# One maximum and one copy of 1024 columns for both heads of a step, over two adjacent PSUM banks

## The chip, the cores and the metric

The kernel runs on one core of a Trainium2 chip. Its time is that of the device from start to end, in microseconds (us). Five engines work side by side, each through its own list of instructions, and meet only at semaphores: TensorE (PE; its weight loads are shown apart as PEld), VectorE (DVE), ScalarE (ACT), GpSimd (POOL) and SyncE (SP), which issues transfers.

## The reference

The program is a block of cross-attention followed by a mixture of experts, all in 32 bits, on 32 batches of 128 rows of 256 values.

```python
q = hidden_states @ Wq; k = encoder_hidden_states @ Wk; v = encoder_hidden_states @ Wv   # 16 heads of 64
scores = jnp.einsum('bhsd,bhkd->bhsk', q, k) * scale
probs = jax.nn.softmax(scores, axis=-1)
out = jnp.einsum('bhsk,bhkd->bhsd', probs, v)
...
x = x + jnp.tanh(g_xattn[0]) * _L0_xattn_ref(_layernorm(x, axis=-1), ctx_768, ...)
x = x + jnp.tanh(g_ffn[0]) * _L0_ffn_ref(_layernorm(x, axis=-1), ...)    # top 2 of 8 experts
```

## The kernel before

The attention stage goes through 8 groups `g` of 4 batches (512 rows). A group has 8 steps `j`, each for a pair of heads; `u = 8g + j` numbers the steps. The change lies in these 64 steps. The stage of the experts behind them (from L1029 on) isn't touched.

PE's list for step `u` is: Q (six matmuls, L591 to L593, into a bank of `proj`), K (five, L599 to L603), V (five, L471 to L475), the scores of `u` (L514, the two heads taking turns, `score[0]` and `score[1]`), the transposes of the probabilities of `u - 1` (L488, first head 0 into `probT[0]`, then head 1 into `probT[1]`), and the product with the values for `u - 2` (L501). Some steps have more jobs behind that: O0 and O1 in step 1 (the output projection of the group before), XA and XB in step 2 (transposes of `xn2`, L539), LG in step 3, PR in step 4, T0 and T1 in step 7 (L560, the tables of the routing). Group 0 has none of these jobs. Group 7 has no V in steps 6 and 7.

The jobs take the two banks of `proj` in turn. `take_bank` makes a job wait until the job two places ahead of it has been copied out. So where a step has only Q, K and V, the V of a step waits for the copy of its own Q, which ACT makes (`q_sb`, L705, counted in the trace as L675). Q of step 3 waits for ACT's copy of XA, and K of step 5 for DVE's copy of PR (`ranks`, L876). T1 waits for the one-hot rows that POOL builds after `route_slots` (L227 to L230).

DVE's list for a step is: copy of V (`v_sb`, L911), low part of an attention result (`aT_l`, L760), the two maxima (L919, one for each head), the two copies of the transposed probabilities of the step before (L886), then for each head a wait for ACT's exponentials, a reciprocal (L947) and a multiplication (L949). ACT's list is: `q_sb`, `k_sb`, `aT_h`, then four exponentials for head 0 and four for head 1 (L722), each head behind a wait for its maximum. The order of all lists is written out by hand, and the waits alone decide when each instruction starts.

Of the kernel before, what the change touches and what calls it, by code (L numbers as in the profile page):

```python
# [5 lines left out]
P = 128  # L6
# [9 lines left out]
GB = 4  # L16
NG = B // GB
TOK = GB * S
# [42 lines left out]
def jobs_of(has_prev, has_next):  # L61
    out = []
    for j in range(NP):
        out += [("Q", j), ("K", j)]
        if has_next or j < NP - V_AHEAD:
            out += [("V", j)]
        if has_next and j == NP - 1:
            out += [("FA", 0), ("FB", 0)]
        if has_prev:
            out += [(m, 0) for m in MISC_PREV.get(j, [])]  # L70
    return out
# [47 lines left out]
def attention(nc, ctx, sem, x_v, out_v, xn2_v, xn2_dram, ctxT, g_x, g_f, wq, wk, wv, wo, bo, gateT, fc1T, fc2, shared):  # L119

    f32, f32r, i32, u32 = mybir.dt.float32, mybir.dt.float32r, mybir.dt.int32, mybir.dt.uint32
    ALU, ACT, AX = mybir.AluOpType, mybir.ActivationFunctionType, mybir.AxisListType.X

    def sb(name, shape, dt=f32):
        return ctx.enter_context(nc.sbuf_tensor(name, shape, dt))
# [29 lines left out]
    pT = sb("pT", [P, 2, 2, TOK])  # L155
# [8 lines left out]
    negmax = sb("negmax", [P, 2, 8])  # L164
# [14 lines left out]
    def ps(name):  # L179
        return ctx.enter_context(nc.psum_tensor(name, [P, TOK], f32))  # L180

    proj = [ps("proj0"), ps("proj1")]
    score = [ps("score0"), ps("score1")]
    probT = [ps("probT0"), ps("probT1")]
    av = [ps("av0"), ps("av1")]

    (
        s_consts, s_wo_in, s_c_in, s_x_in, s_xr_in, s_small_in, s_zeros_out, s_w_hi,
        s_w_lo, s_tanh, s_bias_o, s_zrow, s_q_ready, s_k_ready, s_v_ready, s_s_ready, s_pt_ready,
        s_av_ready, s_o_ready, s_xt_ready, s_lg_ready, s_pr_ready, s_tb_ready, s_f_ready, s_at_hi,  # L190
        s_f_hi, s_q_done, s_k_done, s_v_done, s_pt_done0, s_pt_done1, s_at_split, s_f_split, s_negmax,
        s_exp, s_p_ready, s_o_done, s_xa_done, s_xb_done, s_lg_done, s_pr_done, s_tb_done, s_stats1,
        s_rstd1, s_xn_ready, s_stats2, s_rstd2, s_xn2_ready, s_mask_ready, s_gdiff, s_gexp,
        s_slot_ready, s_onehot0, s_onehot1, s_onehot_last, s_token, s_cv_ready, s_ck_ready, s_xr_ready, s_x1_out, s_xn2_out, s_w_rest,
# [2 lines left out]
        "consts", "wo_in", "c_in", "x_in", "xr_in", "small_in", "zeros_out", "w_hi",  # L197
        "w_lo", "tanh", "bias_o", "zrow", "q_ready", "k_ready", "v_ready", "s_ready", "pt_ready",
        "av_ready", "o_ready", "xt_ready", "lg_ready", "pr_ready", "tb_ready", "f_ready", "at_hi",
        "f_hi", "q_done", "k_done", "v_done", "pt_done0", "pt_done1", "at_split", "f_split", "negmax",  # L200
        "exp", "p_ready", "o_done", "xa_done", "xb_done", "lg_done", "pr_done", "tb_done", "stats1",
        "rstd1", "xn_ready", "stats2", "rstd2", "xn2_ready", "mask_ready", "gdiff", "gexp",
        "slot_ready", "onehot0", "onehot1", "onehot_last", "token", "cv_ready", "ck_ready", "xr_ready", "x1_out", "xn2_out", "w_rest",
# [250 lines left out]
    def _(pe):  # L454
# [27 lines left out]
        def transpose_probs(u, j):  # L482
            for hh in range(2):
                pe.wait_ge(s_p_ready, 2 * u + hh + 1)
                if not isinstance(u, int) or u > 0:
                    pe.wait_ge((s_pt_done0, s_pt_done1)[hh], u)
                for b in range(GB):
                    last = nc.tensor.transpose(probT[hh][:, b * P:(b + 1) * P], probs[j % 2][:, hh * GB + b, :], ident[:, :])  # L488
                last.then_inc(s_pt_ready, 1)

        def weigh_values(u, j, v_needed):

            pe.wait_ge(s_v_done, v_needed)
            if not isinstance(u, int) or u > 1:
                pe.wait_ge(s_at_split, u - 1)
            pe.wait_ge(s_pt_done0, u + 1)
            pe.wait_ge(s_pt_done1, u + 1)
            for b in range(GB):
                for hh in range(2):
                    cols = slice((j % 4) * P + hh * DH, (j % 4) * P + (hh + 1) * DH)  # L500
                    last = mm(av[j % 2][hh * DH:(hh + 1) * DH, b * P:(b + 1) * P], v_sb[:, j // 4, b, cols],  # L501
                              pT[:, j % 2, hh, b * P:(b + 1) * P], start=True, stop=True)
            last.then_inc(s_av_ready, 1)
# [125 lines left out]
        def wait_warm(count):  # L629
            keep_warm(nc, av[1], wk_h[:, 0:P], wk_h[:, 0:TOK], count)  # L630

        def finish():

            u = 8 * NG
            transpose_probs(u - 1, NP - 1)
            weigh_values(u - 2, NP - 2, u)
            weigh_values(u - 1, NP - 1, u)
            for half in range(2):
                pe.wait_ge(s_tb_done, 2 * NG - 1 + half)
                project_out(proj[half], NG, 2 * half)  # L640
            for half in range(2):
                pe.wait_ge(s_xn2_ready, NG + half)
                pe.wait_ge(s_exp, 16 * NG)
                for k in range(DK):
                    for b in range(2):
                        last = nc.tensor.transpose(score[half][:, (2 * k + b) * P:(2 * k + b + 1) * P],
                                                   xn2[:, 2 * half + b, k * P:(k + 1) * P], ident[:, :])
                last.then_inc(s_xt_ready, 1)
                if half == 0:
                    pe.wait_ge(s_at_split, 8 * NG)  # L650
                wait_warm(3)
                pe.wait_ge(s_xa_done, NG + half)
                pe.wait_ge((s_pt_done0, s_pt_done1)[half], 8 * NG)
                for b in range(2):
                    for k in range(DK):
                        last = mm(probT[half][:, b * E:(b + 1) * E], xn2T[:, k, (2 * half + b) * P:(2 * half + b + 1) * P],
                                  gate_sb[:, k, :], start=(k == 0), stop=(k == DK - 1))
                last.then_inc(s_lg_ready, 1)
                wait_warm(6)
            misc("PR", av[0], NG)  # L660
            wait_warm(24)
            for half in range(2):
                pe.wait_ge(s_o_done, 2 * NG - 1 + half)
                misc(f"T{half}", proj[half], NG)
# [8 lines left out]
    def _(act):  # L673
# [26 lines left out]
        def iteration(g, has_prev, has_next):  # L700
            jobs = jobs_of(has_prev, has_next)
            for j in range(NP):
                u = 8 * g + j
                act.wait_ge(s_q_ready, u + 1)
                high(q_sb[:, :], bank_of(("Q", j), jobs)[:, :], SCALE).then_inc(s_q_done, 1)  # L705
                act.wait_ge(s_k_ready, u + 1)
                high(k_sb[:, :], bank_of(("K", j), jobs)[:, :]).then_inc(s_k_done, 1)

                if j > 2 or (has_prev and j < 2):
                    attention_high(u - 3, j - 3)  # L710
                if has_next and j == NP - 1:
                    for k in range(DK):
                        act.wait_ge(s_f_ready, 2 * g + 3 + k)
                        high(xT_h[:, k, :], bank_of(("FA" if k == 0 else "FB", 0), jobs)[:, :]).then_inc(s_f_hi, 1)
                if has_prev and j == 4:
                    act.wait_ge(s_gdiff, g)
                    nc.scalar.activation(gexp[:, :], gdiff[:, :], ACT.Exp).then_inc(s_gexp, 1)
                for hh in range(2):
                    act.wait_ge(s_negmax, 2 * u + 1 + hh)
                    for b in range(GB):  # L720
                        c = hh * GB + b
                        last = nc.scalar.activation(probs[j % 2][:, c, :], score[hh][:, b * P:(b + 1) * P], ACT.Exp,  # L722
                                                    bias=negmax[:, j % 2, c:c + 1], accum_out=sums[:, j % 2, c:c + 1])
                    last.then_inc(s_exp, 1)
                    if hh == 0 and has_prev and j == 2:
                        act.wait_ge(s_xt_ready, 2 * g - 1)
                        high(xn2T[:, 0, :], bank_of(("XA", 0), jobs)[:, :]).then_inc(s_xa_done, 1)
                    if hh == 0 and has_prev and j == 1:
                        attention_high(u - 2, j - 2)
# [24 lines left out]
    def _(dve):  # L754
        me = Steps(dve, s_dve_self)
        V = nc.vector
# [124 lines left out]

        def probs_out(u, j):

            for hh, pt_done in enumerate((s_pt_done0, s_pt_done1)):
                dve.wait_ge(s_pt_ready, 2 * u + 1 + hh)
                V.tensor_copy(pT[:, j % 2, hh, :], probT[hh][:, :]).then_inc(pt_done, 1)  # L886

        def residual_start(g):
            dve.wait_ge(s_xr_ready, g)
# [12 lines left out]
        def iteration(g, has_prev, has_next):  # L902
            jobs = jobs_of(has_prev, has_next)
            for j in range(NP):
                u = 8 * g + j
                if ("V", j) in jobs:
                    n = (j + V_AHEAD) % NP
# [6 lines left out]
                if has_prev and j == 2:  # L914
                    dve.wait_ge(s_rstd2, g)
                    normalise(xn2, x1, mv2, rstd2, s_xn2_ready)
                for hh in range(2):
                    dve.wait_ge(s_s_ready, 2 * u + 1 + hh)
                    V.tensor_reduce(negmax[:, j % 2, hh * GB:(hh + 1) * GB],  # L919
                                    score[hh][:, :].rearrange("p (i k) -> p i k", i=GB), axis=AX, op=ALU.max,  # L920
                                    negate=True).then_inc(s_negmax, 1)
                if has_next and j == NP - 1:
                    for k in range(DK):
                        dve.wait_ge(s_f_hi, 2 * g + 3 + k)
# [19 lines left out]
                for hh in range(2):  # L944
                    c = slice(hh * GB, (hh + 1) * GB)
                    dve.wait_ge(s_exp, 2 * u + 1 + hh)
                    n = me.mark(V.reciprocal(rsum[:, c], sums[:, j % 2, c]))  # L947
# [396 lines left out]
```

## Time and profile before

| | us |
|---|---|
| median of 3 runs | 1044.95 (1043.86 to 1045.88) |
| the profiled execution, its own time | 1039.82 |
| its span, first to last instruction | 1038.1 |
| PE busy | 993.9 (96%) |
| DVE busy | 682.9 (66%) |
| ACT busy | 477.9 (46%) |
| POOL busy | 482.6 (46%) |

The attention stage fills the first 606 us or so; its end is finished by 650 us, and the experts run from there. A busy PE is one on which some matmul runs. In the rows of the trace, what stands in brackets at the end is the idle time of that engine just before the instruction, and what ended it.

### The profile page before, as it was taken

The page shows a single profiled execution, that of the slowest core. Times are in us where ns is not written, and L with a number is a line of the kernel's source. Part 1 is how long each engine was busy: PE and PEld are TensorE (multiplying, and loading weights), DVE is VectorE, ACT ScalarE, POOL GpSimd, SP SyncE. Part 2 cuts the span into 40 slices and gives each one's busy share as a digit, 9 for nine tenths or more (in the row PEclk, how much of TensorE's full clock was granted, in tenths as well). Part 3 has the DMA queues.
Part 4 walks back from the last instruction along what each step waited for, and adds up shares of the span by engine and source line. Part 5 has one row for each costly group of instructions (what it writes and reads, how often), then busy time and mean ns, then how long its engine had stood idle before and what let it go on. Part 6 is the DMA issues. An engine that isn't in the chain of part 4 may idle for free. (4 is left out here: it accounts for less than half of the span.)

```text
span 1038.1 us, 21103 instructions
## 1 busy us (share of the span) xinstructions
PE 993.9 (96%) x7314; PEld 855.4 (82%) x7314; DVE 682.9 (66%) x1607; ACT 477.9 (46%) x1502; POOL 482.6 (46%) x498
## 2 busy tenths in 40 slices
PE   6999999999999999999999997999999999999995
PEld 5778878878878778878878786799999899999995
DVE  5886895885885885885886866444455555444552
ACT  3664553553553553653553541344353544435351
POOL 7521071071071170270270153385858567585856
PEclk9999999999999999999999998999999999999998
DMA  9201110120020020021002001425345262523525
GB/s 247 84 9 54 42 48 13 40 61 7 34 61 20 20 61 33 8 61 56 4 0 61 3 1 41 133 37 132 61 107 127 62 147 35 132 56 102 122 55 66
DMA packets 49948, 63.42 MB, mean 61 GB/s; under 512 B 5976, under 2 KB 41714, under 8 KB 49906
## 3 DMA queue, kind: packets, MB, share of 16 engines
q1 hardware_dynamic: 37234, 45.41, 14.0%
q0 software_dynamic: 12672, 17.47, 10.0%
q8 instruction: 25, 0.41, 0.2%
q14 instruction: 17, 0.14, 0.0%
HBM read 46.45 MB, written 16.78 MB: 61 GB/s over the span
## 5 line engine op out<-in xcount | busy, mean ns | idle before, releaser
L1252 ACT ACTIVATE hid<-up,b 128x512 f32<-128x512 f32 x128 | 88.0, 687 | 86.2 <-PE up L1203 86.2
L722 ACT ACTIVATE work<-score,negmax 128x128 f32<-128x128 f32 x256 | 90.2, 379 | 80.6 <-DVE negmax L919 80.6
L1131 POOL DMA_INDIRECT out_dram<-eo,index_e x64 | 106.4, 1663 | 19.5 <-issue 18.9
L722 ACT ACTIVATE probs_odd<-score,negmax 128x128 f32<-128x128 f32 x256 | 90.2, 380 | 51.6 <-DVE negmax L919 51.6
L343 POOL TENSOR_SCALAR var<-mv 128x4 f32<-128x4 f32 (+1 forms) x17 | 3.8, 226 | 219.8 <-DVE mv L774 212.3
L1304 DVE TENSOR_TENSOR eo_raw<-down,b 128x256 f32<-128x256 f32 x64 | 25.9, 425 | 121.1 <-PE down L1217 121.1
L1297 DVE TENSOR_TENSOR hid_l<-hid,hid_h 128x512 fp32r<-128x512 f32 x128 | 88.7, 693 | 4.4
L675 ACT ACTIVATE q_sb<-proj 128x512 f32<-128x512 f32 x64 | 38.7, 604 | 108.9 <-PE proj L593 108.9
L1295 DVE CAST hid_h<-hid 128x512 fp32r<-128x512 f32 x128 | 54.7, 427 | 47.9 <-ACT hid L1252 46.2
L1260 ACT ACTIVATE eo<-eo_raw,gate_e 128x256 f32<-128x256 f32 x64 | 30.9, 506 | 118.1 <-DVE eo_raw L1304 118.1
L919 DVE TENSOR_REDUCE negmax<-score 128x4 f32<-128x512 f32 x128 | 81.9, 681 | 2.1 <-PE score L514 2.1
L514 PEld LDWEIGHTS score<-k_sb,q_sb 64*128 64x128 f32 x1024 | 63.0, 189 | 24.6 <-issue 24.6
L886 DVE COPY pT<-probT 128x512 f32<-128x512 f32 x128 | 81.9, 682 | 0.0
L1119 POOL DMA_INDIRECT rows<-xn_rows,index_e x64 | 67.8, 1060 | 25.1 <-issue 19.1
L514 PE MATMUL score<-k_sb,q_sb 64*128 64x128 f32 x1024 | 75.3, 287 | 1.5 <-issue 1.5
L911 DVE COPY v_sb<-proj 128x512 f32<-128x512 f32 x62 | 42.5, 686 | 47.8 <-PE proj L475 47.8
L527 PE MATMUL proj<-w_split,aT_h 128*128 128x256 f32 x256 | 73.2, 286 | 0.2 <-DVE aT_l L760 0.2
L528 PE MATMUL proj<-w_split,aT_h 128*128 128x256 f32 x256 | 72.4, 283 | 0.0
L529 PE MATMUL proj<-w_split,aT_l 128*128 128x256 f32 x256 | 72.4, 283 | 0.0
L1215 PE MATMUL down<-w_h,hid_h 128*128 128x256 f32 x256 | 71.6, 280 | 0.0
L1215 PE MATMUL down<-w_split,hid_h 128*128 128x256 f32 x256 | 71.4, 279 | 0.0
L1216 PE MATMUL down<-w_l,hid_h 128*128 128x256 f32 x256 | 70.9, 277 | 0.0
(217 smaller groups left out, 3067.2 us busy)
## 6 DMA issues: line engine op xcount, KB each, us to landing
w_raw<-fc1T_dram SPq DMA_DIRECT2D x9, 1024.0 KB, 5.3
w_raw<-fc_dram SPq DMA_DIRECT2D x9, 1024.0 KB, 9.3
rows<-x_dram SPq DMA_DIRECT2D x16, 512.0 KB, 4.6
out_dram<-rows SPq DMA_DIRECT2D x8, 512.0 KB, 3.0
xn_rows<-rows SPq DMA_DIRECT2D x8, 512.0 KB, 2.9
c_raw<-ctxT_dram SPq DMA_DIRECT2D x8, 256.0 KB, 3.9
c_raw<-ctxT_dram SPq DMA_DIRECT2D x16, 128.0 KB, 4.5
b<-fc2b_dram SPq DMA_DIRECT2D x9, 128.0 KB, 8.4
```

The lines of the kernel that those rows point to most:

```text
L514: last = mm(score[hh][:, t], q_sb[r, t], k_sb[r, t], start=True, stop=True)
L527: mm(o, aT_h[:, j, t], wo_h[:, j, :], start=(j == 0), stop=False)
L528: mm(o, aT_h[:, j, t], wo_l[:, j, :], start=False, stop=False)
L529: last = mm(o, aT_l[:, j, t], wo_h[:, j, :], start=False, stop=(j == NP - 1))
L722: last = nc.scalar.activation(probs[j % 2][:, c, :], score[hh][:, b * P:(b + 1) * P], ACT.Exp, bias=negmax[:, j % 2, c:c + 1], accum_out=s ...
L886: V.tensor_copy(pT[:, j % 2, hh, :], probT[hh][:, :]).then_inc(pt_done, 1)
L919: V.tensor_reduce(negmax[:, j % 2, hh * GB:(hh + 1) * GB], score[hh][:, :].rearrange("p (i k) -> p i k", i=GB), axis=AX, op=ALU.max, negat ...
L1131: pool.indirect_dma_start(out=out_rows[:, :], out_offset=bass.IndirectOffsetOnAxis(ap=index_e[par][:, half * GB + i:half * GB + i + 1], ax ...
L1215: mm(o, hid_h[:, k, t], w2_h[par][:, k, :], start=(k == 0), stop=False)
L1216: mm(o, hid_h[:, k, t], w2_l[par][:, k, :], start=False, stop=False)
L1252: nc.scalar.activation(hid[m % 2][:, :], up[m % 2][:, :], ACT.Relu, bias=b1[par][:, m:m + 1]).then_inc(s_hid, 1)
L1297: V.tensor_tensor(hid_l[:, m, :], hid[m % 2][:, :], hid_h[:, m, :].bitcast(f32), ALU.subtract).then_inc(s_hid_split, 1)
```

## The change

`score` and `probT` become one PSUM tensor each, of two adjacent banks. The two maxima of a step become one instruction over both banks, the two copies of the transposed probabilities become one, and the semaphores go with them: the maximum waits for the scores of both heads, all exponentials wait for that one maximum, the copy waits for the transposes of both heads. What PE and ACT execute stays the same.

```diff
-    score = [ps("score0"), ps("score1")]
-    probT = [ps("probT0"), ps("probT1")]
+    score_pair = ctx.enter_context(nc.psum_tensor("score", [P, 2, TOK], f32))
+    probT_pair = ctx.enter_context(nc.psum_tensor("probT", [P, 2, TOK], f32))
+    score, probT = ([pair[:, n] for n in range(2)] for pair in (score_pair, probT_pair))
...
                 if not isinstance(u, int) or u > 0:
-                    pe.wait_ge((s_pt_done0, s_pt_done1)[hh], u)
+                    pe.wait_ge(s_pt_done, u)
...
+                act.wait_ge(s_negmax, u + 1)
                 for hh in range(2):
-                    act.wait_ge(s_negmax, 2 * u + 1 + hh)
...
-            for hh, pt_done in enumerate((s_pt_done0, s_pt_done1)):
-                dve.wait_ge(s_pt_ready, 2 * u + 1 + hh)
-                V.tensor_copy(pT[:, j % 2, hh, :], probT[hh][:, :]).then_inc(pt_done, 1)
+            dve.wait_ge(s_pt_ready, 2 * u + 2)
+            V.tensor_copy(pT[:, j % 2, :, :], probT_pair[:, :, :]).then_inc(s_pt_done, 1)
...
-                for hh in range(2):
-                    dve.wait_ge(s_s_ready, 2 * u + 1 + hh)
-                    V.tensor_reduce(negmax[:, j % 2, hh * GB:(hh + 1) * GB],
-                                    score[hh][:, :].rearrange("p (i k) -> p i k", i=GB), axis=AX, op=ALU.max,
-                                    negate=True).then_inc(s_negmax, 1)
+                dve.wait_ge(s_s_ready, 2 * u + 2)
+                V.tensor_reduce(negmax[:, j % 2, :], score_pair[:, :, :].rearrange("p s (i k) -> p (s i) k", i=GB),
+                                axis=AX, op=ALU.max, negate=True).then_inc(s_negmax, 1)
```

On DVE, a plain step before, with the semaphore that each instruction waits for:

```order
L911 COPY v_sb<-proj 128x512 [waits a_av_ready,a_v_ready]
L760 TENSOR_TENSOR aT_l<-av,aT_h 128x512 [waits a_at_hi]
L919 TENSOR_REDUCE negmax<-score 128x4 [waits a_s_ready] x2
L886 COPY pT<-probT 128x512 [waits a_pt_ready] x2
L947 RECIPROCAL rsum<-sums 128x4 [waits a_exp]
L949 TENSOR_TENSOR work<-work,rsum 128x512 [waits a_dve_self]
L947 RECIPROCAL rsum<-sums 128x4 [waits a_exp]
L949 TENSOR_TENSOR work<-work,rsum 128x512 [waits a_dve_self]
```

The same step on DVE in the changed kernel, whose lines are numbered one to three lower:

```order
L910 COPY v_sb<-proj 128x512 [waits a_av_ready,a_v_ready]
L760 TENSOR_TENSOR aT_l<-av,aT_h 128x512 [waits a_at_hi]
L917 TENSOR_REDUCE negmax<-score 128x8 [waits a_s_ready]
L885 COPY pT<-probT 128x1024 [waits a_pt_ready]
L944 RECIPROCAL rsum<-sums 128x4 [waits a_exp]
L946 TENSOR_TENSOR work<-work,rsum 128x512 [waits a_dve_self]
L944 RECIPROCAL rsum<-sums 128x4 [waits a_exp]
L946 TENSOR_TENSOR work<-work,rsum 128x512 [waits a_dve_self]
```

Two pairs of instructions have become one each; what stands before and behind them is as it was.

On ACT, the exponentials of a step before, and the copies of the next step that are queued behind them:

```order
L722 ACTIVATE work,sums<-score,negmax 128x128 [waits a_negmax]
L722 ACTIVATE work,sums<-score,negmax 128x128 x3
L722 ACTIVATE work,sums<-score,negmax 128x128 [waits a_negmax]
L722 ACTIVATE work,sums<-score,negmax 128x128 x3
L675 ACTIVATE q_sb<-proj 128x512 [waits a_q_ready]
```

The same place on ACT in the changed kernel:

```order
L722 ACTIVATE work,sums<-score,negmax 128x128 [waits a_negmax]
L722 ACTIVATE work,sums<-score,negmax 128x128 x7
L675 ACTIVATE q_sb<-proj 128x512 [waits a_q_ready]
L675 ACTIVATE k_sb<-proj 128x512 [waits a_k_ready]
L697 REGISTER_ALU
```

The eight exponentials now stand behind one wait instead of two, and `q_sb` of the next step still stands behind all eight.

## Rows read from the trace of the kernel before

**Rows 1.** The page's first part: engines, busy us, share, instructions

```profile
PE 993.9 (96%) x7314; PEld 855.4 (82%) x7314; DVE 682.9 (66%) x1607; ACT 477.9 (46%) x1502; POOL 482.6 (46%) x498
```

**Rows 2.** PE's waits, 95 to 606 us: total us, times, longest

```profile
PE proj L471 <- ACT q_sb L675: 4.0, 6, 0.7
...
PE proj L591 <- ACT work L675: 2.0, 7, 0.3
```

**Rows 3.** DVE groups by shape: busy us, mean ns of one, idle before

```profile
L919 DVE TENSOR_REDUCE negmax<-score 128x4 f32<-128x512 f32 x128 | 81.9, 681 | 2.1 <-PE score L514 2.1
L886 DVE COPY pT<-probT 128x512 f32<-128x512 f32 x128 | 81.9, 682 | 0.0
...
L938 DVE TENSOR_TENSOR table<-proj,table 128x128 f32<-128x128 f32 x14 | 4.0, 286 | 5.8 <-PE proj L560 5.8
```

**Rows 4.** Timelines (start us, us) of a plain step, group 3, steps 0 and 1

```profile
308.62 0.39 PE L471 MATMUL proj<-wv_h,cv_h 128*128 128x512 f32 x1
...
309.96 0.69 DVE L911 COPY v_sb<-proj 128x512 f32<-128x512 f32 x1 [1.41 <-PE proj L475]
...
311.16 1.28 DVE L919 TENSOR_REDUCE negmax<-score 128x4 f32<-128x512 f32 x2
...
314.68 0.60 ACT L675 ACTIVATE q_sb<-proj 128x512 f32<-128x512 f32 x1
...
315.62 0.39 PE L471 MATMUL proj<-wv_h,cv_h 128*128 128x512 f32 x1
```

**Rows 5.** Timelines of group 0: first matmul of V in steps 1, 2, 3, 7

```profile
30.38 0.49 PE L471 MATMUL proj<-wv_h,cv_h 128*128 128x512 f32 x1 [1.43 <-ACT q_sb L675]
...
37.08 0.50 PE L471 MATMUL proj<-wv_h,cv_h 128*128 128x512 f32 x1 [0.65 <-ACT q_sb L675]
...
44.20 0.39 PE L471 MATMUL proj<-wv_h,cv_h 128*128 128x512 f32 x1
...
72.47 0.39 PE L471 MATMUL proj<-wv_h,cv_h 128*128 128x512 f32 x1
```

**Rows 6.** Timeline of DVE in group 0, steps 1 and 3

```profile
32.92 1.29 DVE L919 TENSOR_REDUCE negmax<-score 128x4 f32<-128x512 f32 x2 [0.39 <-PE score L514]
...
45.95 0.66 DVE L911 COPY v_sb<-proj 128x512 f32<-128x512 f32 x1
```

**Rows 7.** Timelines of ACT and PE, steps 2 and 3: the copy of XA

```profile
263.59 0.61 ACT L675 ACTIVATE work<-proj 128x512 f32<-128x512 f32 x1
...
264.25 0.50 PE L591 MATMUL proj<-xT_h,w_split 128*128 128x512 f32 x1 [0.29 <-ACT work L675]
```

**Rows 8.** Timelines of ACT, DVE and PEld, steps 4 and 5

```profile
280.21 0.21 ACT L722 ACTIVATION_READ_ACCUMULATOR work<-score,negmax 128x1 f32 x1
...
280.60 0.17 DVE L947 RECIPROCAL rsum<-sums 128x4 f32<-128x4 f32 x1
...
281.41 0.28 DVE L876 COPY ranks<-proj 128x128 f32<-128x128 f32 x1
...
281.75 0.19 PEld L599 LDWEIGHTS proj<-ck_h,wk_h 128*128 128x128 f32 x1
```

**Rows 9.** Timelines of DVE and PE, steps 5 and 6

```profile
284.45 0.69 DVE L911 COPY v_sb<-proj 128x512 f32<-128x512 f32 x1 [0.28 <-PE proj L475]
...
285.66 1.28 DVE L919 TENSOR_REDUCE negmax<-score 128x4 f32<-128x512 f32 x2
...
290.11 0.40 PE L471 MATMUL proj<-wv_h,cv_h 128*128 128x512 f32 x1
```

**Rows 10.** Timelines of PE and POOL, step 7: V, the last one-hot row, T1

```profile
297.97 0.50 PE L471 MATMUL proj<-wv_h,cv_h 128*128 128x512 f32 x1 [0.69 <-ACT q_sb L675]
...
304.45 0.57 POOL L230 TENSOR_SCALAR rows<-iota,hl,gates 128x64 f32<-128x64 f32 x1
...
305.13 1.13 PE L560 MATMUL proj<-rows,work 128*128 128x128 f32 x8 [0.45 <-issue]
```

**Rows 11.** Timeline of PE at the end of attention: the last transposes of head 1

```profile
608.45 0.66 PE L488 MATMUL probT<-ident,probs_odd 128*128 128x128 f32 x4 [0.16 <-DVE probs_odd L949]
```

More of the change, by code:

```diff
@@ L190, in attention @@
         s_av_ready, s_o_ready, s_xt_ready, s_lg_ready, s_pr_ready, s_tb_ready, s_f_ready, s_at_hi,
-        s_f_hi, s_q_done, s_k_done, s_v_done, s_pt_done0, s_pt_done1, s_at_split, s_f_split, s_negmax,
+        s_f_hi, s_q_done, s_k_done, s_v_done, s_pt_done, s_at_split, s_f_split, s_negmax,
         s_exp, s_p_ready, s_o_done, s_xa_done, s_xb_done, s_lg_done, s_pr_done, s_tb_done, s_stats1,
@@ L199, in attention @@
         "av_ready", "o_ready", "xt_ready", "lg_ready", "pr_ready", "tb_ready", "f_ready", "at_hi",
-        "f_hi", "q_done", "k_done", "v_done", "pt_done0", "pt_done1", "at_split", "f_split", "negmax",
+        "f_hi", "q_done", "k_done", "v_done", "pt_done", "at_split", "f_split", "negmax",
         "exp", "p_ready", "o_done", "xa_done", "xb_done", "lg_done", "pr_done", "tb_done", "stats1",
@@ L495, in weigh_values @@
                 pe.wait_ge(s_at_split, u - 1)
-            pe.wait_ge(s_pt_done0, u + 1)
-            pe.wait_ge(s_pt_done1, u + 1)
+            pe.wait_ge(s_pt_done, u + 1)
             for b in range(GB):
@@ L652, in finish @@
                 pe.wait_ge(s_xa_done, NG + half)
-                pe.wait_ge((s_pt_done0, s_pt_done1)[half], 8 * NG)
+                pe.wait_ge(s_pt_done, 8 * NG)
                 for b in range(2):
```

## The prediction

> **What bounds the kernel now.** I read the busy shares first: PE is busy for 96% of the span [rows 1], so time is gained or lost only where PE waits. Then PE's own waits in the attention stage. They are few and short: 6 times V waits for ACT's `q_sb` (0.69 us each), 7 times Q of step 3 waits for ACT's copy of XA (0.29 each) [rows 2]. DVE has spare time there, so what it is given back is worth little by itself. The question is who releases PE at these places, and how far from waiting PE is at the others. That is read in the timelines of single steps.
>
> In a plain step [rows 4] V starts at 308.62, DVE's maxima at 311.16, and the next V at 315.62, which waited for nothing. Behind this runs a chain that isn't seen as a wait: first maximum, eight exponentials, `q_sb` of the next step, release of the next V. Here `q_sb` starts at 314.68 and is ready at 315.28. The next V's weight load stands about 0.23 ahead of its matmul, at about 315.39. So the chain is spare by about 0.1 us only. Group 0 shows the same chain where it does bound: from the first maximum at 32.92 [rows 6] to V at 37.08, which waited [rows 5], 4.16 us. In that form V's first matmul holds PE 0.11 longer (0.50 instead of 0.39), since its weights can't be loaded ahead [rows 4, 5].
>
> **What the change costs.** *The merged maximum.* No row shows 1024 columns. A maximum of 512 takes 0.681; 128 columns of another PSUM operation take 0.286 [rows 3], so 384 columns more cost 0.395, or 0.527 for 512, and the merged one should take 1.21. The bounds: 1.19 at one column per ns, and 1.36 if nothing is shared. The exponentials of head 0 were released after 0.68 and are released after 1.21: **0.53 us later in each of 64 steps** (0.51 to 0.68). Head 1's stand in line behind them, so the whole group of eight, and `q_sb` behind it, move by 0.53. The chain from the start of the maximum to V becomes 4.16 + 0.53 = 4.69.
>
> *What DVE gets back.* Two maxima start 1.28 - 0.68 = 0.60 apart [rows 4], though each lasts 0.68; of these 0.60, some 0.53 are columns. So each merge frees 0.06, and two of them 0.12 per step, 8 us over 64 steps, in an engine that isn't the bound. The Trainium skill ("Perfetto Trace Analysis", Optimizing Scalar/DVE Operations) gives about 125 ns of overhead for a DVE operation on PSUM and says that grouping helps if the engine is saturated, but that breaking instructions up helps where an unsaturated one causes bubbles on others. By its 125 ns, DVE would get back 0.25 per step, 16 us in all; the trace's spacing gives half of that; and its second half speaks against this change.
>
> *The wait for both heads.* The scores of the two heads take turns on PE, so the second is ready less than 0.1 after the first, and the merged copy of `probT` starts behind the merged maximum, when both transposes are done. I price both at nothing inside the stage.
>
> Now the places, each with what PE loses.
>
> - *Group 0, +3.4.* V of step 1 comes 0.6 later (0.53, and 0.07 for the second head's scores). From V to the maxima 2.54 pass [rows 4], 2.65 when V itself waited. So six steps of 2.65 + 4.69 = 7.34 replace those from 30.38 to 72.47 [rows 5], which took 42.09: 44.04, +1.95. In step 3 DVE comes late as it is: `v_sb` starts at 45.95 [rows 6], 1.75 behind its V at 44.20 [rows 5], where a plain step has 1.34. To these 0.41 come 0.53 from the step before, less about 0.28 by which that V is late itself: +0.66. The same at step 7, in front of Q of group 1: +0.2. Sum 0.6 + 1.95 + 0.66 + 0.2 = 3.4.
> - *Step 0 to 1 of groups 1 to 7, +0.34 each.* 311.16 + 4.69 = 315.85 instead of 315.62, and 0.11 for the weights.
> - *Step 2 to 3, +0.53 each.* The copy of XA stands on ACT behind the four exponentials of head 0, and PE already waits for it: it ends at 264.20, Q starts at 264.25 [rows 7]. Both move whole.
> - *Step 4 to 5, inside the group.* The fourth exponential of head 0 ends at 280.42, the reciprocal ran at 280.60, the copy of PR 0.81 behind it [rows 8]. Now the exponentials end at 280.95, the reciprocal runs at 280.99, PR is out at 282.09, and the weights of K, which were loaded from 281.75, come at 282.13. With 0.23 less for the load that ran ahead and 0.11 for the stall, K is 0.27 later, and so is V.
> - *Steps 5 to 7, inside the group.* DVE was free 0.28 before `v_sb` at 284.45 [rows 9]; its second reciprocal now comes 0.53 later, so `v_sb` starts at 284.75, +0.30. The next V: 285.96 + 4.69 = 290.65 instead of 290.11, +0.54 and 0.11. At step 7, V was waiting already [rows 10]: +0.18 from DVE and 0.53, +0.71.
> - *What takes it back.* T1 waits for POOL: the last one-hot row ends at 305.02, T1 starts at 305.13 [rows 10]. Without POOL it would follow T0 by about 0.73 less. POOL's rows hang on DVE's `route_slots` in step 5 alone, and these come +0.30 - 0.12 = +0.18. So all that PE lost in steps 4 to 7 (0.71) lies under this wait, but for **+0.18** per group. If that cover were gone, each group would cost 0.53 more, 3.2 us for six.
> - *Group 7 and the end, +1.9.* It has the 0.34 and the 0.53, but no such cover: the last transposes wait for DVE [rows 11]. DVE's second reciprocal of step 6 is about 0.86 late (0.33 and 0.53), the exponentials of step 7 then 1.39, less about 0.34 spare: the last transposes of head 1 and what hangs on them come 1.05 later than before.
>
> Sum: 3.4 + 6 x (0.34 + 0.53 + 0.18 = 1.05) + 0.87 + 1.05 = **11.6 us**. The experts' stage has none of these instructions and only starts later. Against the profiled execution's own 1039.82 that is 1051.4; the median of the runs lies 5.1 above that execution, and 1044.95 + 11.6 = **1056.5**.
>
> **The rivals.** 0.2%, or 2.1 us, is about what a measurement of this kernel can tell from no change.
>
> *Only the waits that exist grow.* If the 0.1 spare in the plain step is really 0.5 (a release that is faster than the rows' ends suggest), V of step 1 and of the plain steps of group 0 keeps its place: 1.5 in group 0, 7 x 0.53 = 3.7 for XA, 6 x 0.18, and 1 at the end: +7.3, 1052. For it: the ends of PE's rows are modelled. Against: [rows 5] show the chain bounding in two steps of group 0 with the same length.
>
> *Dearer.* If a merged maximum takes 1.36, the 0.53 becomes 0.68 at about 20 places, +3; if POOL's cover is thinner, up to 3 more; if PE's longer pauses lower its granted clock, some more again: 1060 to 1063.
>
> *No change.* ACT is busy for 46% only [rows 1], and 0.53 might vanish in its idle time. Against: it idles before the exponentials, not behind them, where `q_sb` follows at once. Time 1045.
>
> *Faster.* DVE's backlog, not the exponentials, might decide. In steps 4 to 7 it does so in part: `route_slots` would come earlier by two merges, 0.12 by the spacing, up to 0.30 if each frees 0.15 (its whole fixed part, 0.681 - 0.53), and T1 with it. Seven times 0.30 are 2.1 us: 1042.8. It decides only if exponentials released up to 0.53 later cost nothing, so where the merged maximum lasts no longer than 0.68 + 0.30, that is under 0.98, double the column rate of [rows 3]. The Trainium skill's page "VectorE: DVE Perf Modes" (The perf-mode tier table) gives `tensor_reduce` one rate only, which speaks against it; no row here shows another.
>
> **How the numbers follow.** My forecast, 1053.5 to 1059.5: 0.50. Only the existing waits, 1047 to 1053.5: 0.20. Dearer, above 1059.5: 0.17. No change: 0.08. Faster: 0.05. So slower by over 0.2%: 0.87, within: 0.08, faster: 0.05. The range takes in the forecast, most of the cheaper case from 1050 and of the dearer one to 1062.
>
> **What would show it.** In the profile after: one maximum per step near 1.21 us, and the first exponential that much behind its start; PE's wait for `q_sb` no longer in 6 of these places but in nearly all plain steps of group 0 and in steps 1, 6 and 7 of each group; the wait for XA at 0.82 instead of 0.29; T1's wait nearly gone; a group of 8 steps 1.05 us longer; the experts' stage as long as before. I am wrong if V after a plain step still starts without a wait, if the merged maximum is far from 1.21, or if PE's clock shows in it.

## The result, and the profile after

The changed kernel takes 1056.96 us (median of 4 runs, 1055.4 to 1057.49), the kernel before 1044.5 beside it (4 runs, 1043.86 to 1045.88). The ratio is 1.0117, with a 95% interval of 1.0105 to 1.013: 12.5 us slower, where 11.6 was forecast. The profiled execution took 1055.4 us, with a span of 1053.3.

The page's first part, and from its costliest groups the merged instructions and the exponentials (busy us, mean ns of one, and behind the bar the idle time before them):

```profile
PE 1001.8 (95%) x7314; PEld 852.5 (81%) x7314; DVE 679.4 (64%) x1479; ACT 475.7 (45%) x1502; POOL 482.8 (46%) x498
...
L722 ACT ACTIVATE work<-score,negmax 128x128 f32<-128x128 f32 x256 | 90.2, 379 | 95.9 <-DVE negmax L917 95.9
...
L917 DVE TENSOR_REDUCE negmax<-score 128x8 f32<-128x1024 f32 x64 | 77.8, 1216 | 1.0 <-PE score L514 0.9
L885 DVE COPY pT<-probT 128x1024 f32<-128x1024 f32 x64 | 77.8, 1216 | 0.1
```

DVE executes 128 instructions fewer and is busy for 3.5 us less [rows 1]. PE executes as many as before and is busy for 7.9 us more, since a busy PE includes matmuls whose weights come late and those at a lower clock; 3.1 of these us lie within what two executions of the kernel before differ by (993.9 and 997.0). What the change did has to be read from the waits and from single steps, as before.

PE's waits from 95 to 606 us, which answer to [rows 2]:

```profile
PE proj L591 <- ACT work L675: 5.8, 7, 0.8
PE proj L472 <- ACT q_sb L675: 4.4, 12, 0.5
```

and one line of the same view before, which is gone after:

```profile
PE proj L560 <- issue: 2.7, 6, 0.5
```

The wait for XA grew from 2.0 to 5.8 us in the same seven places, 0.54 in each. V waits for `q_sb` in 12 places instead of 6. The wait of T1 (L560) is gone. But all waits that PE shows there add up to about what they did before (10.9 us instead of 10.2), so these lines alone don't give the loss: part of it is in matmuls that are held for less than the view lists, and part was a wait that moved.

A plain step, step 0 of group 4, in the timeline (start, duration, engine). It is the step of [rows 4], which stand under group 3 but are of group 4 too:

```profile
313.74 0.39 PE L472 MATMUL proj<-wv_h,cv_h 128*128 128x512 f32 x1
...
316.28 1.22 DVE L917 TENSOR_REDUCE negmax<-score 128x8 f32<-128x1024 f32 x1
317.53 0.37 ACT L722 ACTIVATE work<-score,negmax 128x128 f32<-128x128 f32 x1 [2.50 <-DVE negmax L917]
...
320.29 0.64 ACT L675 ACTIVATE q_sb<-proj 128x512 f32<-128x512 f32 x1
320.98 0.50 PE L472 MATMUL proj<-wv_h,cv_h 128*128 128x512 f32 x1
```

The merged maximum takes 1.22 us, and the chain from its start to the next V is 320.98 - 316.28 = 4.70. V to V is 7.24, where it was 7.00 [rows 4] (over groups 1 to 6, 7.23 and 7.02), and V's first matmul takes 0.50 instead of 0.39: its weights came with it, not ahead of it.

The V's of group 0, and the DVE multiplication of its first step:

```profile
28.76 2.81 DVE L946 TENSOR_TENSOR work<-work,rsum 128x512 f32<-128x512 f32 x1
29.05 0.50 PE L472 MATMUL proj<-wv_h,cv_h 128*128 128x512 f32 x1 [2.01 <-ACT q_sb L675]
36.77 0.50 PE L472 MATMUL proj<-wv_h,cv_h 128*128 128x512 f32 x1 [1.65 <-ACT q_sb L675]
...
52.08 0.50 PE L472 MATMUL proj<-wv_h,cv_h 128*128 128x512 f32 x1 [0.73 <-ACT q_sb L675]
59.44 0.50 PE L472 MATMUL proj<-wv_h,cv_h 128*128 128x512 f32 x1
66.80 0.50 PE L472 MATMUL proj<-wv_h,cv_h 128*128 128x512 f32 x1
74.18 0.50 PE L472 MATMUL proj<-wv_h,cv_h 128*128 128x512 f32 x1
```

From step 4 on they stand 7.36 to 7.38 apart. V of step 3, at 44.07, comes 7.30 behind that of step 2, and from it to V of step 4 pass 8.01, where 8.00 were forecast (7.34, and 0.66 for DVE, which is late there). V of step 3 and the V's from step 5 on start without a listed wait, yet each first matmul takes 0.50: a chain can bound where no wait is shown.

XA in step 2 of group 3, which answers to [rows 7]:

```profile
267.23 0.37 ACT L722 ACTIVATE work<-score,negmax 128x128 f32<-128x128 f32 x1 [3.69 <-DVE negmax L917]
268.62 0.61 ACT L675 ACTIVATE work<-proj 128x512 f32<-128x512 f32 x1
...
269.28 0.50 PE L591 MATMUL proj<-xT_h,w_split 128*128 128x512 f32 x1 [0.83 <-ACT work L675]
```

Step 7 of that group, which answers to [rows 10]. T0 and T1 are the 16 matmuls of L560:

```profile
303.65 0.50 PE L472 MATMUL proj<-wv_h,cv_h 128*128 128x512 f32 x1 [0.50 <-ACT q_sb L675]
...
309.38 0.58 POOL L231 TENSOR_SCALAR rows<-iota,hl,gates 128x64 f32<-128x64 f32 x1
...
309.19 2.05 PE L560 MATMUL proj<-rows,work 128*128 128x128 f32 x16
311.15 0.47 PE L591 MATMUL proj<-xT_h,w_split 128*128 128x512 f32 x1
```

POOL's last row is ready at 309.96, while T0 still runs, and T1 follows T0 in one stretch. PE is so late by itself that POOL is no longer waited for.

The end of the attention stage, which answers to [rows 11], with the first matmul of the output projection after and before, then PE by the microsecond there (length, PE's busy us and matmuls, granted clock, DMA share, GB/s), then the last copy before the experts:

```profile
616.90 0.66 PE L489 MATMUL probT<-ident,probs_odd 128*128 128x128 f32 x4 [1.29 <-DVE probs_odd L946]
618.29 0.66 PE L489 MATMUL probT<-ident,probs_odd 128*128 128x128 f32 x4 [0.74 <-DVE probs_odd L946]
...
622.42 0.39 PE L527 MATMUL proj<-w_split,aT_h 128*128 128x256 f32 x1
```

```profile
611.64 0.36 PE L527 MATMUL proj<-w_split,aT_h 128*128 128x256 f32 x1 [0.21 <-DVE aT_l L760]
```

```profile
616.00:617.00 1.00, 0.10 (x1) 1.00 0.00 0
617.00:618.00 1.00, 0.55 (x4) 1.00 0.00 0
618.00:619.00 1.00, 0.71 (x6) 1.00 0.00 0
619.00:620.00 1.00, 1.00 (x12) 0.50 0.00 0
```

```profile
659.10 0.29 DVE L1273 TENSOR_TENSOR table<-table,keep 128x128 f32<-128x128 f32 x1 [0.34 <-PEq L102]
```

From the last transposes to the output projection 4.13 us pass; before the change they were 3.19. PE was busy for 1.36 us from 616 to 619, where it had been busy for 1.65 from 606 to 609 before the change. The granted clock then stood at 0.50, the 1.2 GHz level, from 619 to 622 us; it was 1.00 all through this place before.

### The profile page after: what moved, and what is told of

Same layout as the page of the kernel before. It is cut to its first block and busy times, and to the rows that moved or that the text cites. A ratio compares the mean times of both kernels' runs of the same rounds, so it can differ in the third digit from the quotient of the medians.

```text
span 1053.3 us, 20823 instructions
## 1 busy us (share of the span) xinstructions
PE 1001.8 (95%) x7314; PEld 852.5 (81%) x7314; DVE 679.4 (64%) x1479; ACT 475.7 (45%) x1502; POOL 482.8 (46%) x498
## 5 line engine op out<-in xcount | busy, mean ns | idle before, releaser
L722 ACT ACTIVATE work<-score,negmax 128x128 f32<-128x128 f32 x256 | 90.2, 379 | 95.9 <-DVE negmax L917 95.9
L917 DVE TENSOR_REDUCE negmax<-score 128x8 f32<-128x1024 f32 x64 | 77.8, 1216 | 1.0 <-PE score L514 0.9
L885 DVE COPY pT<-probT 128x1024 f32<-128x1024 f32 x64 | 77.8, 1216 | 0.1
L501 PE MATMUL av<-pT,v_sb 128*64 128x128 f32 x1024 | 71.5, 283 | 0.0
```

The lines of the kernel that those rows point to most:

```text
L885: V.tensor_copy(pT[:, j % 2, :, :], probT_pair[:, :, :]).then_inc(s_pt_done, 1)
L917: V.tensor_reduce(negmax[:, j % 2, :], score_pair[:, :, :].rearrange("p s (i k) -> p (s i) k", i=GB), axis=AX, op=ALU.max, negate=True).th ...
```

## The experiments

Each kernel was timed beside the kernel before, whose median was 1045.76 (only the maxima, only the copies, early, late), 1045.39 (the release alone, and the three with XA's copy moved) and 1045.68 (the kernel before again). Gains and losses in us are the ratio less one, times 1045.4; by that measure the changed kernel is 12.2 slower. "The six groups" is the time from Q of group 1 to Q of group 7 in the profiled execution; it is 455.33 before and 461.11 in the changed kernel. It holds six whole groups and nothing of the start and the end, and repeated to 0.3 us when the kernel before was profiled again.

### Only the maxima merged

`splits(j)` gives the ends of the pieces in which the eight blocks of a step go through the maximum: `[8]` is one merged instruction, `[4, 8]` two as before.

```diff
+def splits(j):
+    return [8]
...
+                ends = splits(j)
...
-                    act.wait_ge(s_negmax, 2 * u + 1 + hh)
...
+                        if c == 0 or c in ends:
+                            act.wait_ge(s_negmax, 8 * u + min(e for e in ends if e > c))
...
-                for hh in range(2):
-                    dve.wait_ge(s_s_ready, 2 * u + 1 + hh)
-                    V.tensor_reduce(negmax[:, j % 2, hh * GB:(hh + 1) * GB],
...
+                c0 = 0
+                for c1 in splits(j):
+                    dve.wait_ge(s_s_ready, 2 * u + (1 if c1 <= GB else 2))
+                    V.tensor_reduce(negmax[:, j % 2, c0:c1],
...
+                    c0 = c1
```

> Only the two maxima are merged; the two copies of the transposed probabilities stay apart. Theory (the exponentials are released 0.53 us later, and PE waits for what stands behind them on ScalarE): all of the loss is here, +11 to +13 us on the 1044.5 of the kernel before, so 1055.5 to 1057.5; PE's wait at step 2 (the copy of XA) is 0.83 instead of 0.29. Rival (the merged copy, which waits for both heads' transposes, carries a good part): at most +7, below 1052.

Measured: 1058.74 us, ratio 1.012 (1.0104 to 1.0135), 12.5 us slower; the six groups take 462.64. PE's waits, 95 to 606 us:

```profile
PE proj L476 <- ACT q_sb L680: 5.9, 12, 0.7
PE proj L596 <- ACT work L680: 5.8, 7, 0.8
```

The merged maximum alone gives the whole loss and the whole pattern of waits. V waits somewhat more than in the changed kernel, 0.49 against 0.37 in each of 12 places. That makes 1.5 us, and the six groups are 1.53 longer here than in the changed kernel: so much the merged copies give back.

### Only the copies merged

The maxima use the same `splits`, with `[4, 8]` in every step.

```diff
-            for hh, pt_done in enumerate((s_pt_done0, s_pt_done1)):
-                dve.wait_ge(s_pt_ready, 2 * u + 1 + hh)
-                V.tensor_copy(pT[:, j % 2, hh, :], probT[hh][:, :]).then_inc(pt_done, 1)
+            dve.wait_ge(s_pt_ready, 2 * u + 2)
+            V.tensor_copy(pT[:, j % 2, :, :], probT_pair[:, :, :]).then_inc(s_pt_done, 1)
```

> Only the two copies are merged; the maxima stay apart. Theory: VectorE gets 0.06 us back per step and nothing waits longer inside the stage, so 1043.5 to 1045 (0 to -1 us), with at most 0.5 lost at the end where the copy waits for the second head. Rival (the merged copy carries a good part): +4 or more, 1048.5 and above.

Measured: 1044.44 us, ratio 0.9991 (0.9981 to 1.0): 0.9 us faster, which the interval doesn't tell from nothing. The six groups take 453.95, 1.4 less than before, 0.23 per group. I had allowed for 0.06 of each merge in DVE's list. PE waits in the same places, for `q_sb` 0.25 less in each of six:

```profile
PE proj L564 <- issue: 2.8, 6, 0.5
PE proj L476 <- ACT q_sb L679: 2.5, 6, 0.4
PE proj L595 <- ACT work L679: 2.1, 7, 0.3
```

T1 (now L564) waits for POOL as long as before, and POOL's last row ends 40.54 us behind Q of step 3 in group 3, where it was 40.77. The rows hang on DVE's `route_slots`, whose first two instructions are a sum and a product that run beside POOL. In this kernel, in group 3:

```profile
285.30 0.21 DVE L855 TENSOR_TENSOR place<-ranks,running 128x64 f32<-128x64 f32 x1
285.54 1.20 DVE L857 TENSOR_TENSOR place<-place,mask 128x64 f32<-128x64 f32 x1
```

In the kernel before:

```profile
288.05 1.33 DVE L849 TENSOR_TENSOR place<-ranks,running 128x64 f32<-128x64 f32 x1
289.42 0.23 DVE L851 TENSOR_TENSOR place<-place,mask 128x64 f32<-128x64 f32 x1
```

1.56 became 1.41. So a shift by 0.06 also let the first instruction in ahead of a neighbour on POOL (`cv_d`, from 288.01 before and from 285.32 here), and these 0.15 with the 0.06 are about the 0.23.

Group 0 gives part of the gain back: from V of step 1 to Q of group 1 it takes 48.48 instead of 47.93. Of that, 0.4 lie between V of step 3 and V of step 4 (7.49 instead of 7.09), where DVE is idle for 0.15 and 0.25 us among its statistics. The same 7.46 to 7.49 stand in the two other kernels that merge the copies and keep two maxima in step 3 (late, and copies with XA's copy moved). The profile names no releaser for most of it, and the cause was not traced; the prediction had put the merged copy at nothing.

The "faster" rival of the prediction had the mechanism right, DVE's backlog through `route_slots`, but it decides only while the exponentials aren't late.

### The release alone

Nothing is merged; ACT's exponentials wait for both maxima.

```diff
                 for hh in range(2):
-                    act.wait_ge(s_negmax, 2 * u + 1 + hh)
+                    act.wait_ge(s_negmax, 2 * u + 2)
```

> The kernel before, with two maxima and two copies as they were, but ScalarE waits for both maxima before the first exponential. Nothing is merged; the release alone moves, by the 0.60 us from one maximum's start to the next. Theory (the release of the exponentials sets the loss): at least the loss of the merged maximum, +12 to +15 us, and a wait for the copy of XA of 0.29 + 0.60 = 0.89. Rival (it is the instruction over two banks that costs, by itself or against other engines): under +3.

Measured: 1060.93 us, ratio 1.0142 (1.0127 to 1.0158), 14.8 us slower; the six groups take 465.02. The waits:

```profile
PE proj L591 <- ACT work L675: 6.3, 7, 0.9
PE proj L471 <- ACT q_sb L675: 6.2, 12, 0.7
```

This is the run that isolates the cause: DVE's work is that of the kernel before, to the instruction, and the loss is all there. It is larger than in the changed kernel because two maxima end 1.28 us after the first one starts, the merged one after 1.22, and because the copies give nothing back. A rival by which a reduction over two banks is itself slow, or disturbs PE's writes, is not needed.

### The maximum merged in steps 0 to 3, and in steps 4 to 7

Both are the kernel with only the copies merged, but for one line, so the copies are merged in all steps.

```diff
 def splits(j):
-    return [4, 8]
+    return [8] if j < 4 else [4, 8]
```

> Copies merged in every step, maxima merged in steps 0 to 3 of each group only. Theory: what PE loses ahead of step 4 stays lost: 0.3 at V of step 1 and 0.53 at the copy of XA in each of 7 groups, 5.9, and about 2.2 in group 0: +8 us, 1052.5 (1051 to 1054). Rival (each of the 64 merged maxima costs the same): half of the full loss, +6, and the same as its counterpart in steps 4 to 7.

```diff
 def splits(j):
-    return [4, 8]
+    return [8] if j >= 4 else [4, 8]
```

> Copies merged in every step, maxima merged in steps 4 to 7 of each group only. Theory: inside a group the loss of steps 4 to 7 lies under the wait of T1 for GpSimd's one-hot rows, so only 0.1 to 0.2 per group are left, 1 us for six, 1 in group 0, 1 at the end of the attention stage and up to 1.2 more where PE's clock is granted at half there: +3.2 us, 1047.7 (1046 to 1049.5). Rival (each merged maximum costs the same): +6, 1050.5, as much as in steps 0 to 3.

Measured: early 1053.36, ratio 1.0075 (1.0061 to 1.0089), +7.8 us; late 1048.88, ratio 1.0036 (1.0022 to 1.0049), +3.8 us. The waits of the early kernel:

```profile
PE proj L595 <- ACT work L679: 5.8, 7, 0.8
PE proj L564 <- issue: 2.7, 6, 0.5
PE proj L476 <- ACT q_sb L679: 2.7, 6, 0.5
```

and of the late one:

```profile
PE proj L476 <- ACT q_sb L679: 4.4, 12, 0.5
PE proj L595 <- ACT work L679: 2.0, 7, 0.3
```

The two halves have the waits that the places demand: XA's wait belongs to the early steps, and only the late steps make T1's wait for POOL vanish. Over the six groups, against the kernel with only the copies merged, early costs 4.95 (458.90 - 453.95), late 2.08 (456.03 - 453.95), both together 7.16 (461.11 - 453.95). They add up to 7.03. The early loss is not taken back by T1's wait, because steps 5 to 7 and POOL's work move with it; 4.95 / 6 = 0.83 is about the 0.32 of step 1 and the 0.53 of XA. The late loss is 0.35 per group, of which the merged copies pay back 0.23, which leaves 0.12 against the kernel before. Between Q of step 3 and V of step 7 these groups lose 0.67, and behind V of step 7 they win 0.57 back, where T1 no longer waits for POOL.

### The copy of XA ahead of the exponentials

If late exponentials hurt at XA only because ACT's copy stands behind four of them, the place in ACT's list is what sets the price. The edit is the same in three kernels: the changed one, the one before, and the one with only the copies merged.

```diff
+                if has_prev and j == 2:
+                    act.wait_ge(s_xt_ready, 2 * g - 1)
+                    high(xn2T[:, 0, :], bank_of(("XA", 0), jobs)[:, :]).then_inc(s_xa_done, 1)
                 act.wait_ge(s_negmax, u + 1)
...
-                    if hh == 0 and has_prev and j == 2:
-                        act.wait_ge(s_xt_ready, 2 * g - 1)
-                        high(xn2T[:, 0, :], bank_of(("XA", 0), jobs)[:, :]).then_inc(s_xa_done, 1)
```

In the changed kernel:

> The changed kernel, with ScalarE's copy of XA ahead of the exponentials of step 2 instead of between the two heads. Theory: PE's wait of 0.83 us in front of step 3 goes, with the 0.1 that the restart costs, in 7 groups, and since it lies ahead of step 4 nothing downstream takes it back: 5 to 6.5 us less than the changed kernel, +6 to +7.5 on the kernel before. Rival (PE isn't held there, or the exponentials that now start behind the copy cost as much elsewhere): within 2 us of the changed kernel.

Measured: 1050.17 us, ratio 1.0043 (1.0029 to 1.0057), 7.7 us less than the changed kernel by the two ratios. The wait for XA is gone from its list. The six groups take 455.30, 0.97 less per group. From Q of step 2 to Q of step 3 pass 7.98 instead of 9.05, 1.07 less: the wait of 0.83, and 0.24 more because Q now follows the second transposes of step 2 (XB) without a stop. 0.12 are lost again at V of step 3, whose first matmul takes 0.50 instead of 0.39. The gain of 7.7 lies above the expected 5 to 6.5, and the loss against the kernel before, 4.5, below the expected 6 to 7.5; by the trace seven groups make 6.8, and the rest is within the intervals.

In the kernel before:

> The kernel before, with the same move of the copy of XA. Theory: its wait of 0.29 us and the restart go, 0.35 in 7 groups, -2.5 us (-1.5 to -3). Rival: the exponentials of step 2 start 0.66 later than before, behind the copy, and something behind them waits: no gain or a loss.

Measured: 1040.84 us, ratio 0.9961 (0.9947 to 0.9975), 4.1 us less. The copy and the Q that waited for it:

```profile
260.29 0.60 ACT L675 ACTIVATE work<-proj 128x512 f32<-128x512 f32 x1 [3.33 <-PE proj L539]
...
261.62 0.48 PE L591 MATMUL proj<-xT_h,w_split 128*128 128x512 f32 x1
```

Q starts 0.73 behind the end of the copy, without a wait. The copy doesn't run wholly in idle time: ACT idles for 3.33 us until XA is transposed, and the exponentials, which started 3.75 behind `k_sb` before, now start 4.42 behind it (in group 3), 0.67 later. That costs little: from Q of step 2 to Q of step 3 pass 0.54 less (the wait of 0.29, and 0.25 for the stop itself), and V of step 3, which now starts with late weights, loses 0.12 again. By the trace the edit gives 2.4 us over the six groups (452.91), 0.40 each. Seven groups make 2.8; the measured 4.1 is above the expected 1.5 to 3, and the other 1.3 lie within the interval.

In the kernel with only the copies merged:

> The kernel before with merged copies of the transposed probabilities, two maxima, and the copy of XA ahead of the exponentials of step 2. Theory: both gains add, -1 and -2.5: -3.5 us (-2 to -4.5), faster than both kernels. Rival: the two share one slack and give no more than one of them, -2.5 at most.

Measured: 1040.84 us, ratio 0.9954 (0.994 to 0.9967), 4.8 us less, a little more than the expected 2 to 4.5: faster than both kernels of this case. The six groups take 451.47, 1.44 less than with the edit in the kernel before. In the time of the whole kernel these two aren't told apart.

### The kernel before again

> The kernel before once more, unchanged, for a second profile of it. In the first one the experts' stage took 389.4 us and the first V of step 1 started at 30.38 us; in every other kernel profiled here, whose experts' stage and start are the same code, these are 394 to 396.5 and about 29.05. If the first profile was a fast execution of the experts' stage (which is how its span lay 5 us under the median), this one shows about 395 and 29, with a span of 1042 to 1045. Rival: the changes themselves lengthen the experts' stage by 5 us, by where the attention stage ends; then this one shows 389.4 again.

Measured: 1046.71 us, ratio 1.0009 (0.9997 to 1.0021), span 1045.4. The six groups take 455.61, and PE's waits are those of [rows 2], line for line. What differs from the first profile is the experts' stage, whose code no kernel here changes: 389.4 us behind the last copy of the attention stage in the first profile, 396.3 in this one, 394.0 to 396.5 in all other kernels. That is of the size of the 5.1 us between the first profiled execution and the median; the executions that weren't profiled can't be divided into stages. The span, 1045.4, lies a little above the expected 1042 to 1045, and the rival, that the changes lengthen the experts' stage, is refuted. The expectation's remark that the others had V of step 1 at the same time doesn't hold: over the executions it started between 27.6 and 31.7 us, at granted clocks of 0.72 to 1.00 from 20 to 26 us.

A kernel that hands the maxima over in pieces smaller than a bank, to release the exponentials earlier still, was not tried: ACT would read a bank that DVE still reads. So it stays open whether an earlier release than that of the kernel before would be worth anything.

## Why the prediction was right

Direction, cause and size held. By place, against its own steps (inside a group, the means of groups 1 to 6):

| step of the prediction | predicted | measured |
|---|---|---|
| merged maximum | 1.21 | 1.22 |
| chain from maximum to V | 4.69 | 4.70 |
| V of step 1, against its V before | +0.23 and 0.11 | +0.21 and 0.13 |
| Q of step 3 behind XA | +0.53 | +0.54 |
| V of step 5, against Q of step 3 | +0.27 | +0.32 |
| Q of step 3 to V of step 7 | +0.71 | +0.67 |
| Q of step 3 to the next group's Q | +0.18 | +0.10 |
| one group | +1.05 | +0.96 |
| group 0, V of step 1 to Q of group 1 | +2.8 | +3.6 |
| plain steps of group 0 | 7.34 | 7.30 to 7.38 |
| Q of group 7 to the last transposes | +1.92 | +1.80 |
| Q of group 7 to the last copy | +1.92 | +2.35 |

Four terms were mis-sized, and their errors partly cancel.

- **T1's wait as a cover.** The residue was priced by POOL: its rows were to come 0.18 later. In group 3 DVE's part (`hl`) was done 0.09 later, relative to Q of step 3, and POOL then needed 13.76 us for its rows instead of 13.94, so the last row came 0.09 earlier. And the cover was thinner than the 0.73 that the prediction read: from the start of T0 to the next Q now pass 1.96 us instead of 2.49, which is 0.53. PE's own loss of 0.67 is larger than that, and PE became what bounds the step. So the residue is near the forecast by luck: its reason was another, the cover is used up. Any further loss in steps 4 to 7 would now be paid whole.
- **What DVE gets back.** 0.06 per merge is right for the instruction alone. With only the copies merged it was worth 0.23 per group to the six groups, of which about 0.15 came through a neighbour on POOL.
- **Group 0.** 0.8 more than forecast in this execution. The multiplication at 28.76 took 2.81 us instead of 0.69, which made DVE late for step 1; by the period of that step, 7.72 instead of the forecast 7.34, some 0.4 of the 0.8 is that. It isn't part of the change: a multiplication at that place took 3.08 in the kernel before with XA's copy moved, and the changed kernel with that copy moved had none longer than 1.73 there and took 7.30 for this step. The rest lies between V of step 7 and Q of group 1, 6.39 instead of 5.84: 0.55, where the prediction had 0.2. That one is part of the change: it is 6.39 to 6.46 in all five kernels with late exponentials in step 7, 5.81 to 5.84 in the six others. DVE's four normalising instructions, which the transposes ahead of that Q need, start 0.32 behind V instead of 0.02 ahead of it and take 2.26 instead of 1.99.
- **The end.** The last transposes came as forecast, 0.12 less. Behind them 0.94 more passed, 4.13 instead of 3.19, in which PE ran at the 1.2 GHz level for three microseconds; some of it was made up before the last copy. The prediction had lower clocks only in the dearer rival, and at one place it was right. All runs agree on this place: in the five kernels with late exponentials in steps 4 to 7 (the changed one, only the maxima, the release alone, late, and the changed one with XA's copy moved) the granted clock fell to 0.50 around the last transposes, and from these to the output projection passed 4.13 to 4.54; in the six others it stayed at 1.00 and 3.19 or 3.20 passed. That PE's pauses themselves caused the drop was not tested apart from the exponentials.

Taken together by the traces: six groups 5.8, group 0 some 3.6 with 0.5 ahead of it, from V of step 0 to V of step 1 at full clock (7.28, and 6.80 with only the copies merged), the end 2.35. That is 12.2, and the runs gave 12.5.

One of the prediction's signs of being wrong came by its letter: V after a plain step (320.98) still starts without a listed wait. The sign was badly chosen, since the chain bounds there all the same, by 0.21 us and by the 0.50 of the first matmul.

Of the rivals, "only the existing waits grow" needed 0.5 us of slack in the plain step and is refuted by the 7.36 of group 0 and the 7.24 of step 1. "No change" is refuted: ACT's idle time before the exponentials grew, from 80.6 to 95.9 us in front of the even steps' alone, and `q_sb` behind them came later all the same. "Dearer" needed a merged maximum of 1.36, which took 1.22, and had the lower clock right at one place. That breaking work up can be better than grouping it, as the Trainium skill has it for an engine that isn't saturated but makes others wait ("Perfetto Trace Analysis", Optimizing Scalar/DVE Operations), is what the runs show: DVE, busy for 64%, saved 3.5 us, and the kernel lost 12.5.

## What to carry to other kernels

Merging two instructions releases those who wait for the first one later, by what the second half adds to the merged one (here 0.54 us); what the merge saves is less (here 0.07 us of occupation). So price a merge first by who is queued behind the first release and how near that chain is to bounding, and only then by busy time. A wait elsewhere in the loop can cover part of the loss until it is used up; and a short copy that the bounding engine needs can be worth placing ahead of a long row of instructions on its engine, if what it delays there has slack: here it gave 0.54 us per group and cost 0.12.

## What the runs showed of the hardware

- A reduction or a copy of 128 x 512 values of 32 bits from PSUM takes 0.68 us on DVE, one of 128 x 1024 over two adjacent banks 1.22, and the next instruction starts 1.13 after its start (47.39 to 48.52 in group 0). Two instructions of 512 start 0.60 apart and so need 1.20: merging saves 0.07 of occupation.
- Small DVE instructions stretch beside POOL: the sum into `place` took 0.21 or 1.33 us, the product 1.20 or 0.23, by which of them met POOL's `cv_d` instruction of 1.3 us. A 128 x 512 multiplication took 0.69, and 2.81 to 3.17 beside POOL's splitting of weights at the start.
- The same code of the experts' stage took 389.4 us in one execution and 394.0 to 396.5 in ten others. In the fast one PE never waited for `hid`. What sets this was not found.
